# Storing each node pair's features in its own turn of the load-and-store loop, not three turns later

## The reference

```
feat = relu(einsum('nd,ohdk->ohnk', x, W) + b)        # o = 0: self, o = 1: neighbour
att_n = leaky(einsum('hnk,hk->hn', feat[1], a_neigh)) # slope 0.2, 4 heads of 32
edge_w = (att_s[:, row] + att_n[:, col]) * adj_vals
agg = segment_sum(edge_w * feat[1][:, col, :], row)
```

## Time and profile before

| what | before |
|---|---|
| median of 3 runs | 5036.38 us |
| the profiled execution, its own time | 5030.4 us |
| its span | 5028.8 us |
| sorting stage with the pairs | about 144 to 446 us |
| sorting stage without them | about 446 to 760 us |
| VectorE busy in 143.8 to 446.2 us | 295.32 of 302.40 us |
| TensorE busy there | 249.72 us |

### The profile page before, as it was taken

The page is one execution under the profiler, slowest core; times in us unless marked ns, Lnnn a source line. Parts: engine busy times, 40 slices in busy tenths (PEclk is TensorE's granted clock), DMA queues, the critical chain, the costliest instruction groups (busy, mean ns, idle before and its releaser), DMA issues.

```text
span 5028.8 us, 67492 instructions
## 1 busy us (share of the span) xinstructions
PE 3674.9 (73%) x17277; PEld 2816.9 (56%) x17277; DVE 3651.0 (73%) x8530; ACT 2489.6 (50%) x5972; POOL 3615.5 (72%) x4003
## 2 busy tenths in 40 slices
PE   0787764667767676666767678888888888888886
PEld 0676553455545555555555456666666666666664
DVE  4899994666666666666666557777777777777776
ACT  0454224444444444444444356666666666666664
POOL 1567886777777777777777567777777777777774
PEclk9999996888898888989888889999999999999997
DMA  3231003445455555444554556565555665666555
GB/s 103 78 91 53 7 7 93 141 148 148 149 148 153 149 148 150 148 148 148 148 153 146 108 156 172 172 177 176 173 174 174 177 175 172 176 177 175 172 172 114
DMA packets 393065, 710.59 MB, mean 141 GB/s; under 512 B 77542, under 2 KB 233410, under 8 KB 392654
## 3 DMA queue, kind: packets, MB, share of 16 engines
q0 software_dynamic: 161104, 434.80, 31.0%
q1 hardware_dynamic: 231582, 271.44, 17.7%
HBM read 622.28 MB, written 85.27 MB: 141 GB/s over the span
## 4 chain that ended last, share of the span: by engine, by line
POOL 57%; issue 19%; PE 4%; DMA 3%; DVE 1%; ACT 1%; DVEq 0%; ACTq 0%; POOLq 0%
POOL arena L668 30%; POOL arena L680 26%; DMA arena<-d_p,tabS 2%; PE ps L1069 1%; PE ps L1098 1%; DMA arena<-d_t,tabD 1%; PE ps L1047 0%; DVE arena L1547 0%; PE ps L1035 0%; DVE big L1537 0%; PE ps L1080 0%; ACT tabE L900 0%; ACT arena L815 0%; POOL arena L660 0%; ACT tabE L887 0%
## 5 line engine op out<-in xcount | busy, mean ns | idle before, releaser
L680 POOL DMA_INDIRECT arena<-d_p,tabS x1628 | 1571.0, 965 | 548.5 <-issue 488.1
L668 POOL DMA_INDIRECT arena<-d_t,tabD x1628 | 1554.9, 955 | 509.4 <-issue 493.8
L1047 PE MATMUL ps<-arena 128*128 128x256 f32 x3256 | 999.9, 461 | 639.2 <-ACT arena L815 523.0
L815 ACT ACTIVATE arena<-arena,tabE 128x256 f32<-128x256 f32 x1628 | 693.4, 496 | 1034.2 <-DMA arena<-d_t,tabD 1034.0
L1047 PEld LDWEIGHTS ps<-arena 128*128 128x128 f32 x3256 | 706.3, 227 | 863.7 <-DVE big L1402 565.4
L1069 PE MATMUL ps<-arena 128*128 128x256 f32 x3256 | 870.4, 397 | 180.9 <-DVE big L1537 171.1
L1080 PE MATMUL ps<-big,tabE 128*128 x3256 | 809.1, 387 | 93.9 <-DVE arena L1547 82.5
L1537 DVE SCALAR_TENSOR_TENSOR big<-big,tabK,ps 128x256 f32 x1628 | 774.5, 476 | 93.7 <-DVE big L1537 83.1
L1402 DVE TENSOR_TENSOR big<-big,ps 128x256 f32 x1628 | 681.4, 419 | 200.9 <-DVE big L1402 191.4
L1069 PEld LDWEIGHTS ps<-arena 128*128 128x128 f32 x3256 | 595.2, 194 | 407.2 <-DVE big L1537 227.1
L915 ACT ACTIVATE arena<-arena 128x1024 f32<-128x1024 f32 x407 | 430.2, 1057 | 740.3 <-DVE arena L1547 740.1
(11 more groups left out here) (249 smaller groups left out, 4073.4 us busy)
## 6 DMA issues: line engine op xcount, KB each, us to landing
arena<-d_loc SPq DMA_DIRECT2D x407, 256.0 KB, 4.0
arena<-d_t,tabD POOLq DMA_INDIRECT x1628, 2.8
arena<-d_p,tabS POOLq DMA_INDIRECT x1628, 3.4
arena<-in_xT_dram SPq DMA_DIRECT2D x96, 256.0 KB, 3.6
d_t<-arena SPq DMA_DIRECT2D x49, 256.0 KB, 2.1
d_xp<-arena SPq DMA_DIRECT2D x49, 256.0 KB, 2.6
arena<-d_xp SPq DMA_DIRECT2D x49, 256.0 KB, 4.0
d_x<-arena SPq DMA_DIRECT2D x49, 256.0 KB, 2.6
```

Source lines behind the costliest of these rows:

```text
L668: e.indirect_dma_start(out=GB[g][:, k, :], out_offset=None, in_=d_t, in_offset=bass.IndirectOffsetOnAxis(ap=tabD[:, j, k:k + 1], axis=0)). ...
L680: e.indirect_dma_start(out=G1[j % 8][:, k, :], out_offset=None, in_=d_p, in_offset=bass.IndirectOffsetOnAxis(ap=tabS[:, j, k:k + 1], axis= ...
L815: a = e.activation(GB[q][:, k, :], GB[q][:, k, :], ACT.Copy, scale=tabE[:, j - 1, 1, k:k + 1])
L1047: m = e.matmul(PS[4 + 2 * q + k // 2][:, (k % 2) * 256:(k % 2) * 256 + 256], OH[q][:, k, :], GB[(g - 1) % 4][:, k, :], start=True, stop=True)
```

## The change

SP's loop makes 49 turns in place of 52. In turn j it still issues load j+2 first, and then it waits for the gates of pair j itself (`a_gm >= j + 1`) and stores pair j. Before, it waited in turn j for those of pair j-3 and stored that one. The semaphores of the stores, the buffers and all other engines' code are the same; `done(j + 2, NP)` is the same condition as before, written with a helper.

```diff
             def load(j, g, i):
-                if j + 2 < NP:
+                if not done(j + 2, NP):
                     loadt("a", XT0, j + 2, g + 2)
-                q = j - 3
-                if q >= 0:
-                    waitn(e, "a_gm", q + 1)
-                    e.dma_start(pair(d_t, q), TS[q % 4]).then_inc(S(f"a_ts{q % 4}"), 16)
-            drive(e, NP + 3, 4, load, tail=5)
+                waitn(e, "a_gm", j + 1)
+                e.dma_start(pair(d_t, j), TS[g % 4]).then_inc(S(f"a_ts{g % 4}"), 16)
+            drive(e, NP, 4, load, tail=5)
```

## The result

The kernel with the change takes 5243.23 us, the median of four runs from 5239.44 to 5246.05; the kernel before, with one more run beside it, 5037.07. The ratio is 1.0407, with a 95% interval of 1.0389 to 1.0425: 206 us slower, where 175 (5212) was forecast, and 13 us above the range. The profiled execution took 5231.43 us, with a span of 5229.9; it is 12 us under the median, and its granted clock over the whole span was 0.903 where the four timed runs had 0.891 to 0.896.

The account below looks back on a forecast made before the run. VectorE was taken to set the sort's pace, 6.32 us a step. Late loads (+125) and slow clock (+54) gave +179, on 5030.4 (5209) or the 5036.4 median (5215), so 5212 was said; range 5150 to 5230.

Parts of the forecast that it names:

- A late load per pair from 3 to 48: Sorting stage: load q+3 waits behind pair q's gates, giving some 46 TensorE waits of 3 to 4 us.
- The links of the loop: One sorting step: feature matmuls, L992, ScalarE's copy, gates, store, load, TensorE's restart; 6.06 + 2.98 = 9.04 us.
- 9.04 us at full clock: Sorting step with TensorE's clock at 1.00: 9.04 us in place of 6.32, +125 us in sum.
- the restart after the issue: Sorting step: TensorE restarts 2.98 us after SP issues the load.
- the start of L990: Sorting step: the 16 matmuls (L992 before the change) start 1.61 us after the feature matmuls start.
- The clock term: Sorting steps: TensorE idles some 3.5 us and restarts slowly, 1.2 us in nearly every step, 54 us in sum.
- The upper bound is 45 x 1.45 = 65: Sorting steps: the most that slow TensorE restarts were said to cost, 1.45 us a step on L992.
- The one-in-four: Clock cost if one restart in four is slow, as in the sort's second part: 45 x 0.3 = 14 us.
- The start: First late load: load 3 goes out behind store 0, at 158.15, and pair 3 starts at 161.13.
- One for one to the end: Behind the sort: time lost in the sort is lost at the kernel's end, later stages only shifted; +179 us.
- The full-clock rival: Sort: late loads at full clock, or one slow restart in four, 125 to 139 us over, 5155 to 5169; chance 0.25.
- The worse rival: Sort: VectorE or the transfers join the loop, for instance load at 3.3 and all of 1.45 paid; 5241, chance 0.07.

Follow-up runs that it names:

- e6: Changed kernel with ScalarE multiplying by the gates of pair j-2 before the copy L781, not behind it; 5727.37 us, ratio 1.009 to the kernel before.
- e9: Changed kernel with ScalarE multiplying by the gates of pair j-2 before the Relu of pair j; 5673.81 us against 5676.58 for the kernel before.
- e5: Changed kernel with load j+3 issued ahead of store j, behind the wait for pair j's gates; 5863.1 us against 5676.32 for the kernel before.
- e2_fill: Changed kernel with 20 unused matmuls before each TensorE wait for the load of pairs 3 to 48; 5917.49 us against 5743.59 for the kernel before.
- e8b_fill30: Changed kernel with 30 unused matmuls before each TensorE wait for the load of pairs 3 to 48; 5818.0 us, ratio 1.0261 to the kernel before.
- e1_lag1: Kernel before with SP storing pair j-1 in turn j in place of pair j-3; 5742.23 us against 5743.59 for the kernel before.

## Why the prediction was right in kind and short in size

1. *A late load per pair from 3 to 48, in a loop that closes once a step.* Shown: 46 waits, 24 with half the pairs, none with a lead of one turn or with the loads on another engine's queue.
2. *The links of the loop.* Shown by e6, which takes L990 and the copy out, and e9, which opens it. e5, which takes the 0.41 of one issue out, agrees, but its 16 us hardly stand clear of the noise.
3. *9.04 us at full clock.* Right: 9.08 is the median with the gap filled, and 15 steps of e2_fill lie at 8.97 to 9.34. Of the small terms, the restart after the issue was 3.10 for 2.98 on average and the start of L990 1.57 for 1.61.
4. *The clock term*, "I take 1.2 in nearly every step", "The upper bound is 45 x 1.45 = 65". This is the step that failed, by its size. The step was 10.87 - 9.04 = 1.83 longer than at full clock; of that the feature matmuls carry 0.54 on average and L990 1.22, together 1.76 a step, or 79 us in place of 54 and above what I had called the bound. I had priced a slow restart as either L992's 1.45 or the feature matmuls' 1.17, and both lie in the loop, one behind the other; together they can cost 1.16 + 1.56 = 2.7. Eight steps paid about that, one 2.3, and the other 36 paid 1.3 to 1.6, some on L990 alone and many on both. The rows for both were in front of me. The one-in-four was misread as well: it counts all of the restarts of the second part, 16 of them after gaps of 0.5 to 0.8 us. Of the 37 after more than 2 us, 13 were slow.
5. *The start.* Pair 3 restarted at 163.09 where 161.13 was forecast, as store 0 went out at 159.58 and not at 157.74: the first chunk's matmuls, L990 at 154.31, took 3.15 us in this execution where L992 took 1.85 in that of before, both after an idle gap of 1.37. That is 2.0 us. Together: 45 x 0.63 + 2.0 = 30 more for pair 48 (652.0 for 621.9). That the result lies 31 over the forecast is in part a coincidence: some 8 of the 30 are given back behind pair 48, so that the span grew by 201.1 for 179, and the median of the timed runs lies 12 above the profiled execution, where 5212 has 3.
6. *One for one to the end.* Right within 4 us: 205.2 at the table, 201.1 in the span.
7. *The full-clock rival* (125 to 139 over) is what e8b_fill30 comes near: 141 us over its kernel before. The worse rival, 5241, hit the time within 2 us, but by luck: it had the load land 0.4 later and the clock cost 1.45, and the loads landed 0.1 later (3.0 us), while the clock cost 1.76.

The Trainium skill, page "TensorE: Matmul & The Clock Gate", section "HAM oscillation — how this bites in real kernels", has the clock lost at every burst that a DMA wait separates from the last. The changed trace agrees: TensorE idled 2.9 to 4.1 us before every restart, and no step is under 10.34 us. With most gaps at 1.6 us in e2_fill it was no longer every burst, but 29 of 44. The Trainium skill, page "DMA: Bandwidth & Descriptors", section "Anatomy of one DMA — SWDGE (gpsimd) path", gives about 2.0 us and the bytes at 436 GB/s, by which 256 KB take 2.6 us, an estimate for GpSimd's path; the trace has 3.0 us for this load, which SP issues.

What is open: why the slow stretch creeps forward until a step of 11.7 comes, why some loads of e8b_fill30 are late, and why the other chips are slower in the gathers. None of these was tried.

## What to carry to other kernels

On a queue that issues in order, count for each load which wait now stands ahead of it, and how long before its use that wait ends: here the lead could shrink from three turns (18 us) to one (5.8 us) at no cost, and the last turn cost all. If the load gates the work that releases the wait, the loop closes once per step and its length is the new step. When the new step leaves TensorE idle for microseconds, price everything on it in the loop at 1.2 GHz, for the bound; not one operation of it.

## What the runs showed of the hardware that I had not expected

- The slow clock came after idle gaps of only 1.3 to 1.6 us (L993 3.23 us for 1.85, e2_fill), though gaps of 2.2 us often kept the fast one in the kernel before, and with some 0.6 us left nearly all steps were fast (0.99). The gap alone does not decide: in e2_fill gaps of 1.5 to 1.7 us were followed by both, and the first chunk's matmuls, after the same 1.37 us, ran fast in one kernel and slow in the other.
- Thirty added matmuls per step, whose results nobody reads, took 62 us off the changed kernel's time.
- The same program took 5037 us on one chip and 5676 and 5744 us on others, with the sort nearly unchanged (6.53 us a step in e1_lag1 and 6.32 in e9b_gatesfirst, for 6.32).
